# First stage of a decoder layer on one core: rotary rows gathered at half width and turned between key products, eight value blocks given places of their own

## The chip, the cores and the metric

The kernel runs on 1 core of a Trainium2 chip. The metric is the device time of one execution in microseconds (us). A core has TensorE (PE, with its weight loads as PEld), VectorE (DVE), ScalarE (ACT), GpSimd (POOL) and SyncE (SP); each works through its own instructions in order, and they wait for each other by semaphores. DMA queues are fed by SP, ACT and POOL.

## The reference

A decoder layer on 32 sequences of 64 tokens (2048 tokens), hidden size 512, all in float32:

```python
x = x + attention(layernorm(x))                         # 32 heads of 16
x = x + cross_attention(layernorm(x), ctx, pos, mask)   # 32 heads of 128, 8 key/value heads, rotary
x = x + ffn(layernorm(x))                               # 512x512 and sixteen low-rank adapters
# what the first stage of the kernel computes, from ctx alone:
k = (ctx @ Wk).reshape(nb, 64, 8, 128); v = (ctx @ Wv).reshape(nb, 64, 8, 128)
k = k * cos_t[pos] + rotate_half(k) * sin_t[pos]        # cos and sin repeat over the two halves of 128
```

## The kernel before, in words

**Stages.** The first stage (class KeysAndValues) projects the context to rotated keys and to values and writes both to scratch in HBM. The self-attention, the cross-attention (which reads the scratch back) and the adapters follow. Nothing in this change but the first stage and one wait behind it is touched. Every float32 operand of a projection is split: a high part in the matmul's input type (an ACT copy, `_hi`), and the rest (a DVE subtraction, `_lo`). A product is three matmuls per chunk of 128 input channels, hi·hi, hi·lo and lo·hi, over KC = 4 chunks: 12 matmuls of 128x512 (`product3`, L69).

**Blocks.** The 2048 tokens are NB = 4 blocks of 512. A block has KVH = 8 value products (L429; product i is token tile i % 4 and one half of the value columns) and 8 key products (L423; one per head). Block 0 differs from blocks 1 to 3. In block 0 the loads come in, PE makes the values first (`first_values`, L436: four products interleaved chunk by chunk, as the chunks come; then values 4 to 7), then keys 0 and 1, then it transposes the cosine and sine rows of all tokens (L465), and then it makes keys 2 to 7. In blocks 1 to 3, PE alternates a key product and a value product.

**What orders the work around the change.** Everything is written by hand, engine by engine; semaphores tie them.

- SP (L230) issues the loads of context and value weights by chunk in turn, the identity, the other half of the value weights, and after `c_ready` the eight key-weight loads; then, in this order, eight value stores (L256), the context of block 1 (L271), and then a key store and a load of tokens by turns. It waits for `v_copied` before each value store, so what stands behind a value store waits too.
- POOL (L292) gathers the cosine and sine rows by position with sixteen indirect DMAs (L298, 128 tokens each, rows of 256 floats: cos, cos, sin, -sin) once the value weights are there, and then adds the two terms of each rotated key (L304).
- ACT (L332) makes the high parts; then for i = 0 to 7 it copies value block i from PSUM to one of two buffers `v_out` (L330; it waits until the store that last read this buffer is done) and makes the high part of key-weight head i (L320). Then it copies the eight groups of turned rows to `cos_t` and `sin_t` (L345), and makes the high part of context block 1.
- DVE (L394) makes the low parts; then for each key three multiplications by cos and sin (`rotate_terms`, L167 to L171) into one of two buffers `k_out` (it waits until the key store that last read it is done) and into `rb`; in between the low parts of context block 1 (L369).
- A product needs a free PSUM bank. Values 4, 5, 6 and 7 wait for the copies of values 0, 1, 4 and 5 (L430), a key product for the rotation two keys earlier (L424).

Of the kernel before, what the change touches and what calls it, by code (L numbers as in the profile page):

```python
# [173 lines left out]
class KeysAndValues:  # L174


    def __init__(self, nc, m, base, banks, x, norm1, ident, drams, wv1_hi, wv1_lo):
# [17 lines left out]
        v_out = [sb(f"v_out{i}", (148 + 2 * i) * KB, [P, BLOCK]) for i in range(2)]  # L195
        pos = sb("pos", 152 * KB, [P, TILES], mybir.dt.uint32)
# [33 lines left out]
        def sync(sp):  # L230
            for c in range(KC):
                sp.dma_start(c_raw[0][:, c, :], ctx_dram[:, c, 0:BLOCK]).then_inc(c_in0[c], 16)
                sp.dma_start(raw["v"][:, c, 0:BLOCK], wv_dram[:, c, 0:BLOCK]).then_inc(v_raw_in[c], 16)
            sp.dma_start(ident[:, :], ident_dram).then_inc(id_in, 16)
            for c in range(KC):
                sp.dma_start(raw["v"][:, c, BLOCK:NKV], wv_dram[:, c, BLOCK:NKV]).then_inc(v_raw_in[KC + c], 16)
            sp.wait_ge(c_ready, KC)
            for i in range(KVH):
                sp.dma_start(raw["k"][:, :, i * D2:(i + 1) * D2], wk_dram[:, :, i * D2:(i + 1) * D2]).then_inc(k_raw_in[i // 2], 16)
# [9 lines left out]
            def store_keys(b, i):  # L249
                need(sp, k_added, b * KVH + i + 1)  # L250
                sp.dma_start(k_scr[i, ds(b, 1), :, :].rearrange("b p n -> p (b n)"), k_out[i % 2][:, :]).then_inc(k_stored[i % 2], 16)

            def store_values(b, i):
# [3 lines left out]
                             v_out[i % 2][:, :].rearrange("p (g d) -> p g d", d=D2)).then_inc(v_stored[i % 2], 16)  # L257
# [1737 lines left out]
```

## Time and profile before

| | us |
|---|---|
| median of 3 runs (lowest to highest) | 1434.88 (1432.6 to 1436.09) |
| the profiled execution: its own time | 1437.98 |
| its span, first to last instruction | 1436.2 |
| PE busy in the span | 1398.4 (97%) |
| DVE / POOL / ACT busy | 1021.6 / 529.2 / 432.5 |
| stretch of the span that holds block 0 of the first stage | 0 to 65.90 |

Times in the rows are us from the span's start. A matmul's duration in a row is longer than the distance to the next one, since matmuls overlap in the engine; how fast PE goes is read from the distance between starts. An instruction's idle time before it, and what ended it, stand in square brackets.

### The profile page before, as it was taken

How to read it: one execution, taken by the hardware profiler on the slowest of the kernel's cores; microseconds unless marked ns; L12 is line 12 of the kernel's file. 1: busy time of each engine (PE TensorE's matmuls, PEld its weight loads, DVE VectorE, ACT ScalarE, POOL GpSimd, SP SyncE). 2: the span in 40 equal slices, each digit the busy share in tenths (PEclk: the TensorE clock that was granted, in tenths of full speed). 3: DMA queues.
4: the chain of work that ended last, by engine and by line, in shares of the span. 5: the costliest groups of instructions: out<-in, count | busy, mean ns of one | idle time of the engine just before them, and what ended most of it. 6: DMA issues, size and time to landing. Idle time of an engine off the chain costs nothing.

```text
span 1436.2 us, 27963 instructions
## 1 busy us (share of the span) xinstructions
PE 1398.4 (97%) x11616; PEld 1157.3 (81%) x11616; DVE 1021.6 (71%) x1470; ACT 432.5 (30%) x733; POOL 529.2 (37%) x459
## 2 busy tenths in 40 slices
PE   7999999999997889999999999999999999999999
PEld 5788888788886678888888888888888888888787
DVE  3655552788889977777777777767767767778754
ACT  4211133555667333123123123122122122121421
POOL 4322220334443534344344344344344344342231
PEclk9999999999999989999999999999999999999999
DMA  8565330000005102011011011012011012003011
GB/s 248 158 213 167 125 96 8 2 17 25 10 3 148 30 16 75 30 45 46 30 45 51 25 45 59 16 45 60 15 46 59 16 45 60 16 16 115 1 59 59
DMA packets 79116, 84.09 MB, mean 59 GB/s; under 512 B 9824, under 2 KB 50928, under 8 KB 78736
## 3 DMA queue, kind: packets, MB, share of 16 engines
q1 hardware_dynamic: 68976, 63.42, 14.2%
q10 hardware_dynamic: 9216, 16.78, 3.7%
q0 software_dynamic: 800, 2.11, 0.5%
q8 instruction: 94, 1.54, 0.5%
q14 instruction: 30, 0.25, 0.1%
HBM read 59.22 MB, written 23.07 MB: 57 GB/s over the span
## 4 chain that ended last, share of the span: by engine, by line
PE 60%; POOL 3%; DVE 1%; issue 1%; ACT 0%; ACTq 0%
PE p_ps_y L1240 6%; PE p_ps_y L1242 6%; PE p_ps_y L1241 6%; PE p_ps_qk L75 4%; PE p_ps_qk L77 4%; PE p_ps_qk L76 4%; PE p_ps_s L1201 3%; POOL p_wo_lo L1164 3%; PE p_ps_s L1212 2%; PE p_ps_o L75 2%; PE p_ps_s L1242 2%; PE p_ps_s L1241 2%; PE p_ps_s L1240 2%; PE p_ps_o L76 2%; PE p_ps_o L77 2%; PE p_ps_s L1227 2%
## 5 line engine op out<-in xcount | busy, mean ns | idle before, releaser
L1619 POOL TENSOR_TENSOR p_q_rot<-p_q_rot,p_rb 128x512 f32<-128x512 f32 x128 | 167.6, 1309 | 324.7 <-DVE p_rb L171 324.7
L1240 PE MATMUL p_ps_y<-p_wo_hi,p_o_hi 128*128 128x512 f32 x384 | 151.2, 394 | 1.9 <-DVE p_o_lo L1494 1.3
L1241 PE MATMUL p_ps_y<-p_wo_lo,p_o_hi 128*128 128x512 f32 x384 | 149.5, 389 | 0.0
L1242 PE MATMUL p_ps_y<-p_wo_hi,p_o_lo 128*128 128x512 f32 x384 | 149.5, 389 | 0.0
L75 PE MATMUL p_ps_qk<-p_xt_hi,p_wq_hi 128*128 128x512 f32 x312 | 130.3, 418 | 1.0 <-issue 1.0
L999 POOL TENSOR_TENSOR p_pn<-p_p,p_inv 128x512 f32<-128x512 f32 x64 | 66.2, 1066 | 155.2 <-DVE p_inv L889 152.7
L77 PE MATMUL p_ps_qk<-p_xt_hi,p_wq_lo 128*128 128x512 f32 x312 | 122.9, 394 | 0.0
L76 PE MATMUL p_ps_qk<-p_xt_lo,p_wq_hi 128*128 128x512 f32 x312 | 121.9, 391 | 0.0
L1348 ACT ACTIVATE p_pt_hi<-p_ps_s 128x512 fp32r<-128x512 f32 x64 | 38.2, 599 | 255.2 <-PE p_ps_s L1212 255.2
L1503 DVE TENSOR_TENSOR x_sb<-p_ps_y,x_sb 128x512 f32<-128x512 f32 x96 | 66.3, 691 | 68.4 <-PE p_ps_y L1242 67.4
L1354 ACT ACTIVATE p_o_hi<-p_ps_s 128x512 fp32r<-128x512 f32 x64 | 34.8, 595 | 232.2 <-PE p_ps_s L1227 232.2
L304 POOL TENSOR_TENSOR p_k_out<-p_k_out,p_rb 128x512 f32<-128x512 f32 x32 | 44.9, 1402 | 117.7 <-DVE p_rb L171 117.7
L1240 PEld LDWEIGHTS p_ps_y<-p_wo_hi,p_o_hi 128*128 128x128 f32 x384 | 72.1, 188 | 20.0 <-POOL p_wo_lo L1164 3.6
L1625 POOL TENSOR_TENSOR p_v_lo<-p_v_in,p_v_hi 128x512 fp32r<-128x512 f32 x32 | 41.5, 1296 | 116.8 <-ACT p_v_hi L1339 116.8
L1242 PEld LDWEIGHTS p_ps_y<-p_wo_hi,p_o_lo 128*128 128x128 f32 x384 | 72.1, 188 | 15.1
L1241 PEld LDWEIGHTS p_ps_y<-p_wo_lo,p_o_hi 128*128 128x128 f32 x384 | 72.2, 188 | 14.7 <-issue 0.2
L1612 POOL TENSOR_TENSOR p_s<-p_s,p_inv 128x512 f32<-128x512 f32 x64 | 65.6, 1047 | 35.6 <-DVE p_inv L1470 35.6
L169 DVE TENSOR_TENSOR p_q_rot<-p_ps_qk,p_cos_t 128x512 f32<-128x512 f32 x64 | 43.8, 685 | 44.1 <-PE p_ps_qk L77 42.1
L77 PEld LDWEIGHTS p_ps_qk<-p_xt_hi,p_wq_lo 128*128 128x128 f32 x312 | 58.7, 188 | 13.8
L75 PEld LDWEIGHTS p_ps_qk<-p_xt_hi,p_wq_hi 128*128 128x128 f32 x312 | 58.9, 189 | 13.2 <-issue 1.4
L1343 ACT ACTIVATE p_s<-p_s 128x1024 f32<-128x1024 f32 x32 | 34.0, 1062 | 117.7 <-DVE p_s L1462 117.7
L1201 PE MATMUL p_ps_s<-p_k_t,p_q_rot 128*64 128x64 f32 x2048 | 68.2, 226 | 0.5 <-POOL p_q_rot L1619 0.5
(265 smaller groups left out, 3802.2 us busy)
## 6 DMA issues: line engine op xcount, KB each, us to landing
v_scratch<-p_v_out SPq DMA_DIRECT2D x32, 256.0 KB
k_scratch<-p_k_out SPq DMA_DIRECT2D x32, 256.0 KB, 2.1
p_raw<-in_wq SPq DMA_DIRECT2D x32, 256.0 KB, 3.1
p_raw<-in_wo SPq DMA_DIRECT2D x32, 256.0 KB, 2.6
p_k_t<-k_scratch ACTq DMA_DIRECT2D x32, 256.0 KB, 2.6
p_v_in<-v_scratch ACTq DMA_DIRECT2D x32, 256.0 KB, 2.9
x_sb<-in_x SPq DMA_DIRECT2D x16, 256.0 KB, 3.0
out<-p_y SPq DMA_DIRECT2D x16, 256.0 KB, 2.0
```

The costliest lines, as they stand in the source:

```text
L75: nc.tensor.matmul(out, lh, rh, start=(c == 0), stop=False)
L76: nc.tensor.matmul(out, lh, rl, start=False, stop=False)
L77: mm = nc.tensor.matmul(out, ll, rh, start=False, stop=(c == last))
L304: nc.gpsimd.tensor_tensor(k_out[i % 2][:, :], k_out[i % 2][:, :], rb[i % 2][:, :], ALU.add).then_inc(k_added, 1)
L999: nc.gpsimd.tensor_tensor(pn[:, u * PB:(u + 1) * PB, :, :].rearrange("p b j k -> p j b k"), part, scale.unsqueeze(3).broadcast_to([P, HALF ...
L1201: mm = nc.tensor.matmul(ps_s[half][rows, (h // PAIR * UB + j) * SEQ:(h // PAIR * UB + j + 1) * SEQ], q_rot[:, h, cols], k_t[:, cols], star ...
L1240: nc.tensor.matmul(ps_y[t][:, :], oh, w_hi["o"][h][:, :], start=(h == 0), stop=False)
L1241: nc.tensor.matmul(ps_y[t][:, :], oh, w_lo["o"][h][:, :], start=False, stop=False)
L1242: mm = nc.tensor.matmul(ps_y[t][:, :], ol, w_hi["o"][h][:, :], start=False, stop=(h == H - 1))
L1503: nc.vector.tensor_tensor(x[:, tile, :], ps_y[t][:, :], x[:, tile, :], ALU.add).then_inc(y_added, 1)
L1612: nc.gpsimd.tensor_tensor(part, part, inv[:, half * SETS:(half + 1) * SETS].unsqueeze(2).broadcast_to([P, SETS, SEQ]), ALU.mult).then_inc( ...
L1619: nc.gpsimd.tensor_tensor(q_rot[:, h, :], q_rot[:, h, :], rb[:, :], ALU.add).then_inc(q_added, 1)
```

## The change

The table of rotary rows in HBM has 128 floats per position (64 cosines, 64 sines) where it had 256 (each cosine twice, sine and minus sine). The sixteen gathers write 128 floats per token into one tile `rows`, and count on four semaphores, one per block. PE turns the rows of one block with 4 transposes, 16 in all instead of 32, ahead of keys 0, 2, 4 and 6 of block 0. ACT spreads one turned group over both halves of `cos_t` and `sin_t` with four copies of 64x512 (one scaled by -1), 16 copies instead of 8 of 128x512; the copies of groups 1 to 3 stand behind a wait for all eight value stores of block 0 and for the context of block 1.

Value blocks 0 to 7 of block 0 are copied to eight buffers `v_first`, which lie where context block 1's parts are put later. There are four `k_out` buffers instead of two. The first piece of the value weights is loaded by ACT's queue. PE makes the four first hi·hi matmuls of chunk 0 as soon as both high parts are there. On ACT the value copies 0 to 3 come first, and key-weight heads are done two at a time between copies 4 to 7; the key weights are counted on two semaphores of four loads each. On SP, context block 1 is loaded after value store 5.

```diff
+        KOUT = 4
+        k_out = [sb(f"k_out{i}", at * KB, [P, BLOCK]) for i, at in enumerate((50, 60, 62, 146))]
+        rows = sb("rows", 52 * KB, [P, TILES, D2])
...
+        v_first = [sb(f"v_first{i}", (128 + 2 * i) * KB, [P, BLOCK]) for i in range(KVH)]
...
         def sync(sp):
             for c in range(KC):
                 sp.dma_start(c_raw[0][:, c, :], ctx_dram[:, c, 0:BLOCK]).then_inc(c_in0[c], 16)
-                sp.dma_start(raw["v"][:, c, 0:BLOCK], wv_dram[:, c, 0:BLOCK]).then_inc(v_raw_in[c], 16)
+                if c > 0:
+                    sp.dma_start(raw["v"][:, c, 0:BLOCK], wv_dram[:, c, 0:BLOCK]).then_inc(v_raw_in[c], 16)
...
             def first():
                 for i in range(KVH):
                     store_values(0, i)
-                load_context(1)
-                sp.wait_ge(row_copied, 2)
+                    if i == KVH - 3:
+                        load_context(1)
                 for i in range(KVH):
                     store_keys(0, i)
                     load_tokens(i)
...
         def gpsimd(pool):
...
             for t in range(TILES):
-                pool.indirect_dma_start(rows(t), None, table_dram, bass.IndirectOffsetOnAxis(ap=pos[:, t:t + 1], axis=0)).then_inc(row_in, 16)
+                pool.indirect_dma_start(rows[:, t, :], None, table_dram, bass.IndirectOffsetOnAxis(ap=pos[:, t:t + 1], axis=0)).then_inc(row_in[t // TPB], 16)
...
             def copy_values(b, i):
                 need(act, v_done, b * KVH + i + 1)
-                need(act, v_stored[i % 2], (b * (KVH // 2) + i // 2) * 16)
-                nc.scalar.activation(v_out[i % 2][:, :], values_bank(b, i)[:, :], ACT.Copy).then_inc(v_copied, 1)
+                if b > 0:
+                    need(act, v_stored[i % 2], ((b - 1) * (KVH // 2) + i // 2) * 16)
+                nc.scalar.activation(values_out(b, i)[:, :], values_bank(b, i)[:, :], ACT.Copy).then_inc(v_copied, 1)
+
+            def copy_rows(blk):
+
+                act.wait_ge(row_turned, blk + 1)
+                cols, ps = slice(blk * BLOCK, (blk + 1) * BLOCK), ps_r[blk % 2]
+                nc.scalar.activation(cos_t[0:HALF, cols], ps[0:HALF, :], ACT.Copy)
+                nc.scalar.activation(cos_t[HALF:D2, cols], ps[0:HALF, :], ACT.Copy)
+                nc.scalar.activation(sin_t[0:HALF, cols], ps[HALF:D2, :], ACT.Copy)
+                nc.scalar.activation(sin_t[HALF:D2, cols], ps[HALF:D2, :], ACT.Copy, scale=-1.0).then_inc(row_copied, 1)
 
             def first():
+                act.dma_start(raw["v"][:, 0, 0:BLOCK], wv_dram[:, 0, 0:BLOCK]).then_inc(v_raw_in[0], 16)
...
-                for i in range(KVH):
+                for i in range(TPB):
                     copy_values(0, i)
-                    key_weights_hi(i)
-                for n in range(2 * NB):
-                    act.wait_ge(row_turned, n + 1)
-                    dst = (cos_t, sin_t)[n % 2]
-                    nc.scalar.activation(dst[:, (n // 2) * BLOCK:(n // 2 + 1) * BLOCK], ps_r[n % 2][:, :], ACT.Copy).then_inc(row_copied, 1)
+                for i in range(TPB, KVH):
+                    key_weights_hi(2 * (i - TPB))
+                    if i < KVH - 1:
+                        key_weights_hi(2 * (i - TPB) + 1)
+                    copy_values(0, i)
+                copy_rows(0)
+                key_weights_hi(KVH - 1)
+                act.wait_ge(v_first_stored, 16 * KVH)
                 act.wait_ge(c_in, 16)
-                for c in range(KC):
-                    context_hi(1, c)
+                for blk in range(1, NB):
+                    copy_rows(blk)
+                    if blk < NB - 1:
+                        context_hi(1, 2 * (blk - 1))
+                        context_hi(1, 2 * (blk - 1) + 1)
...
             def rotate(b, i):
...
-                need(dve, row_copied, 2 * (b + 1))
+                need(dve, row_copied, b + 1)
                 need(dve, k_added, n - 1)
-                need(dve, k_stored[i % 2], (b * (KVH // 2) + i // 2) * 16)
...
+                need(dve, k_stored[i % KOUT], n // KOUT * 16)
...
             def first_values():
 
+                pe.wait_ge(c_part, 1)
+                pe.wait_ge(part_hi["v"], 1)
+                for i in range(TPB):
+                    nc.tensor.matmul(values_bank(0, i)[:, :], c_hi[0][:, 0, i * P:(i + 1) * P], w_hi["v"][:, 0, 0:BLOCK], start=True, stop=False)
...
+            def turn_rows(blk):
+
+                pe.wait_ge(row_in[blk], 16 * TPB)
+                need(pe, row_copied, blk - 1)
+                for t in range(TPB):
+                    tr = nc.tensor.transpose(ps_r[blk % 2][:, t * P:(t + 1) * P], rows[:, blk * TPB + t, :], ident[:, :])
+                tr.then_inc(row_turned, 1)
 
             def first():
...
-                for i in range(2):
-                    pe.wait_ge(ready["k"], i + 1)
-                    keys(0, i)
                 pe.wait_ge(id_in, 16)
...
-                for i in range(2, KVH):
+                for i in range(KVH):
+                    if i % 2 == 0:
+                        turn_rows(i // 2)
                     pe.wait_ge(ready["k"], i + 1)
                     keys(0, i)
...
-    return np.concatenate([cos, cos, sin, -sin], axis=1)
+    return np.concatenate([cos, sin], axis=1)
```

DVE's first stage keeps its order but for the low parts of context block 1, which come behind rotations 3 to 6 instead of 0 to 3. Behind the stage DVE waits for the stores of three of the four `k_out` buffers where it waited for one of two.

**How instructions move.** On ACT, in block 0 behind the value weights, stood before:

```order
L330 ACTIVATE p_v_out_71<-p_ps_s 128x512 [waits p3_p1_v_done]
L320 ACTIVATE p_wk_hi<-p_raw_k 128x4x128 [waits p3_p1_k_raw_in0]
L330 ACTIVATE p_v_out_72<-p_ps_s 128x512 [waits p3_p1_v_done]
L320 ACTIVATE p_wk_hi<-p_raw_k 128x4x128 [waits p3_p1_k_raw_in0]
L330 ACTIVATE p_v_out_71<-p_ps_s 128x512 [waits p3_p1_v_stored0,p3_p1_v_done]
L320 ACTIVATE p_wk_hi<-p_raw_k 128x4x128 [waits p3_p1_k_raw_in1]
```

and stands now, from the first value copy to the second group of turned rows:

```order
L340 ACTIVATE p_v_first_74<-p_ps_s 128x512 [waits p3_p1_v_done]
...
L340 ACTIVATE p_v_first_77<-p_ps_s 128x512 [waits p3_p1_v_done]
L329 ACTIVATE p_wk_hi<-p_raw_k 128x4x128 [waits p3_p1_k_raw_in0] x2
L340 ACTIVATE p_v_first_78<-p_ps_s 128x512 [waits p3_p1_v_done]
L329 ACTIVATE p_wk_hi<-p_raw_k 128x4x128 [waits p3_p1_k_raw_in0] x2
L340 ACTIVATE p_v_first_79<-p_ps_s 128x512 [waits p3_p1_v_done]
...
L329 ACTIVATE p_wk_hi<-p_raw_k 128x4x128 [waits p3_p1_k_raw_in1]
L340 ACTIVATE p_v_first_81<-p_ps_s 128x512 [waits p3_p1_v_done]
L346 ACTIVATE p_cos_t<-p_ps_y 64x512 [waits p3_p1_row_turned]
...
L329 ACTIVATE p_wk_hi<-p_raw_k 128x4x128 [waits p3_p1_k_raw_in1]
L346 ACTIVATE p_cos_t<-p_ps_y 64x512 [waits p3_p1_row_turned,p3_p1_c_in,p3_p1_v_first_stored]
```

Value copies no longer wait for `v_stored`, two key-weight heads stand ahead of copy 4, and the second group of turned rows has two waits for DMAs. On PE, the rows were turned after two keys, in one piece (ps_y are the banks of the turned rows, ps_s those of the products):

```order
L77 MATMUL p_ps_s<-p_c_hi_67,p_wk_lo 128x512
L465 MATMUL p_ps_y<-ident,p_rows_61 128x128 [waits p3_p1_row_in,p3_p1_id_in]
L465 MATMUL p_ps_y<-ident,p_rows_61 128x128 x7
L465 MATMUL p_ps_y<-ident,p_rows_61 128x128 [waits p3_p1_row_copied]
...
L465 MATMUL p_ps_y<-ident,p_rows_62 128x128 x3
L75 MATMUL p_ps_s<-p_c_hi_67,p_wk_hi 128x512 [waits p3_p1_k_terms,p3_p1_ready_k]
```

and are now turned in four pieces, the first ahead of every key product:

```order
L77 MATMUL p_ps_s<-p_wv_hi,p_c_lo_70 128x512
L486 MATMUL p_ps_y<-ident,p_rows 128x128 [waits p3_p1_row_in0,p3_p1_id_in,p3_p1_v_copied]
L486 MATMUL p_ps_y<-ident,p_rows 128x128 x3
L75 MATMUL p_ps_s<-p_c_hi_68,p_wk_hi 128x512 [waits p3_p1_ready_k]
...
L486 MATMUL p_ps_y<-ident,p_rows 128x128 [waits p3_p1_row_in1]
L486 MATMUL p_ps_y<-ident,p_rows 128x128 x3
L75 MATMUL p_ps_s<-p_c_hi_68,p_wk_hi 128x512 [waits p3_p1_k_terms,p3_p1_ready_k]
...
L486 MATMUL p_ps_y<-ident,p_rows 128x128 [waits p3_p1_row_copied,p3_p1_row_in2]
```

Each piece waits for the gathers of its own block, and the third and fourth for ACT's copies of the first and second.

## Rows read from the trace of the kernel before

**Rows 1.** Stages of the span: busy time of each engine, granted clock, DMA share, GB/s

```profile
core 0: us, PE busy (x) PEld busy (x) DVE busy (x) ACT busy (x) POOL busy (x), PEclk, DMA share, GB/s
0.00:6.69 6.69, 0.00 (x1) 0.03 (x1) 1.53 (x3) 3.17 (x4) 0.95 (x5) 1.00 0.65 201
6.69:24.53 17.84, 17.84 (x72) 14.49 (x72) 7.82 (x12) 8.44 (x15) 7.61 (x8) 1.00 0.94 297
24.53:27.98 3.45, 0.16 (x2) 0.01 (x1) 1.38 (x2) 2.09 (x5) 2.62 (x3) 0.83 0.96 243
27.98:36.18 8.20, 8.20 (x24) 6.52 (x25) 2.08 (x3) 2.62 (x5) 5.68 (x6) 0.66 0.68 187
36.18:41.63 5.45, 5.45 (x26) 4.46 (x24) 0.69 (x1) 1.12 (x2) 0.00 (x0) 1.00 0.56 143
41.63:46.50 4.87, 4.23 (x33) 3.29 (x32) 2.06 (x3) 3.47 (x7) 0.86 (x1) 1.00 0.44 160
46.50:65.90 19.40, 17.27 (x75) 13.27 (x74) 14.90 (x22) 2.96 (x6) 9.10 (x7) 1.00 0.46 150
65.90:240.00 174.10, 174.10 (x790) 143.63 (x789) 90.21 (x150) 39.00 (x69) 38.39 (x30) 1.00 0.41 132
240.00:1436.20 1196.20, 1171.19 (x10605) 971.60 (x10603) 900.94 (x1275) 369.64 (x623) 463.94 (x402) 0.99 0.13 40
```

**Rows 2.** Who PE waited for from 0 to 240: us in total, times, longest

```profile
PE p_ps_s L444 <- DVE p_wv_lo L375: 6.7, 1, 6.7
PE p_ps_s L75 <- ACT p_v_out L330: 3.3, 1, 3.3
PE p_ps_s L75 <- DVE p_rb L171: 2.1, 3, 1.3
PE p_ps_y L465 <- ACT p_cos_t L345: 0.6, 3, 0.3
```

**Rows 3.** Timeline, the first loads on SP, first work on ACT, DVE, PE: start, us

```profile
0.75 0.39 SPq L232 DMA_DIRECT2D p_raw_k<-in_ctx  x1
1.20 0.42 SPq L233 DMA_DIRECT2D p_raw_v<-in_wv  x1
...
3.63 0.63 ACT L309 ACTIVATE p_c_hi<-p_raw_k 128x512 fp32r<-128x512 f32 x1 [1.59 <-DMA p_raw_k<-in_ctx]
5.19 0.63 ACT L315 ACTIVATE p_wv_hi<-p_raw_v 128x512 fp32r<-128x512 f32 x1 [0.93 <-DMA p_raw_v<-in_wv]
...
5.85 0.69 DVE L375 TENSOR_TENSOR p_wv_lo<-p_raw_v,p_wv_hi 128x512 fp32r<-128x512 f32 x1 [0.86 <-ACT p_wv_hi L315]
...
9.79 0.40 PE L445 MATMUL p_ps_s<-p_wv_lo,p_c_hi 128*128 128x512 f32 x1
```

**Rows 4.** Timeline of ACT, value copies and key-weight heads

```profile
17.25 0.60 ACT L330 ACTIVATE p_v_out<-p_ps_s 128x512 f32<-128x512 f32 x1 [2.69 <-PE p_ps_s L446]
...
23.84 0.60 ACT L330 ACTIVATE p_v_out<-p_ps_s 128x512 f32<-128x512 f32 x1 [4.47 <-issue]
24.34 0.62 ACT L320 ACTIVATE p_wk_hi<-p_raw_k 128x512 fp32r<-128x512 f32 x1
24.86 0.59 ACT L330 ACTIVATE p_v_out<-p_ps_s 128x512 f32<-128x512 f32 x1
...
27.32 0.60 ACT L330 ACTIVATE p_v_out<-p_ps_s 128x512 f32<-128x512 f32 x1 [1.36 <-DMA v_scratch<-p_v_out]
```

**Rows 5.** Timeline of PE around the turned rows

```profile
41.63 1.03 PE L465 MATMUL p_ps_y<-ident,p_rows 128*128 128x128 f32 x8
42.91 1.15 PE L465 MATMUL p_ps_y<-ident,p_rows 128*128 128x128 f32 x8 [0.25 <-ACT p_cos_t L345]
```

**Rows 6.** Timeline of DVE, one rotation behind a key store

```profile
60.84 0.69 DVE L169 TENSOR_TENSOR p_k_out<-p_ps_s,p_cos_t 128x512 f32<-128x512 f32 x1 [1.35 <-DMA k_scratch<-p_k_out]
61.54 0.69 DVE L170 TENSOR_TENSOR p_rb<-p_ps_s,p_sin_t 64x512 f32<-64x512 f32 x1
62.25 0.68 DVE L171 TENSOR_TENSOR p_rb<-p_ps_s,p_sin_t 64x512 f32<-64x512 f32 x1
```

**Rows 7.** Timeline of POOL, first and last of the sixteen gathers

```profile
14.78 1.39 POOL L298 DMA_INDIRECT p_rows<-in_table_c,p_pos  x1 [12.76 <-DMA p_raw_v<-in_wv]
...
34.33 0.95 POOL L298 DMA_INDIRECT p_rows<-in_table_c,p_pos  x1 [0.30 <-issue]
```

More of the change, by code:

```diff
@@ L287, in sync @@
             sp.wait_ge(tables_out, 16 * 2 * NB)
+            for i in range(KOUT):
+                sp.wait_ge(k_stored[i], 16 * NB * KVH // KOUT)
+            sp.wait_ge(v_first_stored, 16 * KVH)
             for i in range(2):
-                sp.wait_ge(k_stored[i], 16 * NB * KVH // 2)
-                sp.wait_ge(v_stored[i], 16 * NB * KVH // 2)
+                sp.wait_ge(v_stored[i], 16 * (NB - 1) * KVH // 2)
         def gpsimd(pool):
@@ L294, in gpsimd @@
             pool.wait_ge(pos_in, 16)
-            for n in range(NH * KC):
-                pool.wait_ge(v_raw_in[n], 16)
+            for c in range(KC):
+                pool.wait_ge(v_raw_in[c], 16)
+            pool.wait_ge(v_raw_in[KC], 16 * KC)
             for t in range(TILES):
-                pool.indirect_dma_start(rows(t), None, table_dram, bass.IndirectOffsetOnAxis(ap=pos[:, t:t + 1], axis=0)).then_inc(row_in, 16)
+                pool.indirect_dma_start(rows[:, t, :], None, table_dram, bass.IndirectOffsetOnAxis(ap=pos[:, t:t + 1], axis=0)).then_inc(row_in[t // TPB], 16)
             def body(b):
@@ L303, in body @@
                     need(pool, k_terms, n + 1)
[L304 removed]
+                    nc.gpsimd.tensor_tensor(k_out[i % KOUT][:, :], k_out[i % KOUT][:, :], rb[i % 2][:, :], ALU.add).then_inc(k_added, 1)
             blocks(lambda: body(0), body)
@@ L443, in first_values @@
                         ch, cl, wh, wl = c_hi[0][:, c, tile], c_lo[0][:, c, tile], w_hi["v"][:, c, 0:BLOCK], w_lo["v"][:, c, 0:BLOCK]
-                        nc.tensor.matmul(out, ch, wh, start=(c == 0), stop=False)
+                        if c > 0:
+                            nc.tensor.matmul(out, ch, wh, start=False, stop=False)
                         nc.tensor.matmul(out, ch, wl, start=False, stop=False)
@@ L455, in first @@
                 need(pe, v_copied, TPB)
-                for i in range(2):
-                    pe.wait_ge(ready["k"], i + 1)
-                    keys(0, i)
                 pe.wait_ge(id_in, 16)
-                pe.wait_ge(row_in, 16 * TILES)
-                for n in range(2 * NB):
-                    blk, part = n // 2, n % 2
-                    need(pe, row_copied, n - 1)
-                    for t in range(TPB):
-                        tr = nc.tensor.transpose(ps_r[part][:, t * P:(t + 1) * P], rows(blk * TPB + t)[:, part * D2:(part + 1) * D2], ident[:, :])
-                    tr.then_inc(row_turned, 1)
-                for i in range(2, KVH):
+                for i in range(KVH):
+                    if i % 2 == 0:
+                        turn_rows(i // 2)
                     pe.wait_ge(ready["k"], i + 1)
@@ L923, in _ @@
             need(dve, kv.tables_out, 16 * 2 * NB)
-            need(dve, kv.k_stored[0], 16 * NB * KVH // 2)
+            for stored in kv.k_stored[0:3]:
+                need(dve, stored, 16 * NB * KVH // 4)
             for t in range(TILES):
```

39 lines of the change are left out of this document (19 added, 20 removed).

## The prediction

> **What bounds the kernel now.** I read the stages of the span first. PE is busy 1398 of 1436 us; from 65.90 to 240 it is busy without a gap, and behind 240 it lacks 25 us in places that this change does not touch [rows 1]. So only what PE loses before 65.90, the start of block 1's first key product, can be won, and every us of it should come off the end, since all that follows is released by PE's own progress. Next I read whom PE waited for: four causes before 65.90, none from there to 240 [rows 2]. The reader should lay both over each other, as the stages were cut at PE's events. They add up to 65.90:
>
> - 0 to 6.69: no matmul yet. The first waits for the low part of the value weights [rows 2, 3].
> - 6.69 to 24.53: 72 matmuls (values 0 to 5).
> - 24.53 to 27.98: PE stands still. Value 6 needs the bank of value 4, and ACT's copy of value 4 started only at 27.32, since its buffer was being stored [rows 4].
> - 27.98 to 36.18: 24 matmuls (values 6, 7) in 8.20 us, at a granted clock of 0.66 over the stretch, where 24 at full clock take 5.45 us (36.18 to 41.63, keys 0 and 1) [rows 1]. The clock fell to its lower level, 1.2 GHz, behind the stop.
> - 41.63 to 46.50: the 32 transposes, with some stops for ACT's copies.
> - 46.50 to 65.90: six key products in 19.40 us. Six at full rate are 3 x 5.45 = 16.35. The rest is waiting for DVE's rotations, which wait in turn for a key store to free their buffer, 1.35 us in the row shown [rows 6].
>
> **The change, part by part.** I take each part against this list.
>
> *Start.* The first four matmuls need only high parts now. The one of the weights ends at 5.19 + 0.63 = 5.82, the low part at 5.85 + 0.69 = 6.54, and PE began 0.15 later [rows 3]. That is 0.72 earlier. The weight load leaves first on ACT's queue, not second on SP's: 1.20 - 0.75 = 0.45 earlier. Together 1.2: PE starts at 5.5. Bounds: if the load lands as fast as the context's (3.63 - 0.75 = 2.9 us from issue, where it took 5.19 - 1.20 = 4.0), ACT goes 3.63, 4.26, 4.89 and PE starts at 5.04, a gain of 1.65; if the context's load becomes as slow as the weights' instead, ACT starts at 4.75, ends at 6.01 and PE starts at 6.16, a gain of 0.5. I take the middle, because both loads share the engines either way. PE then runs on: its remaining eight matmuls of chunk 0 wait for a low part about 0.45 earlier than 6.54, when four matmuls are under way. Its first slow matmuls (the spacing turns fast at 9.79, 3.1 us after the start [rows 3]) I leave at the same length.
>
> *Value copies.* Copies 0 to 7 wait for no store. The stop of 3.45 us goes, and the slow patch behind it, 8.20 - 5.45 = 2.75 us. What is late next is the pair of key-weight heads that now stands ahead of copy 4. PE, 1.2 earlier, finishes value 5 at 23.3; for value 6 to start then, ACT must start these two heads by about 21.6 (two at 0.5 spacing and the copy at 0.6). They now need the first four key-weight loads. ACT took the third head at 24.34 with no wait for its load, so that it landed is only proven for 24.34 [rows 4]. DMA moved 297 GB/s to 24.53 [rows 1]; the queue up to the fourth load is 1.0 MB context, 2.1 MB value weights, 0.06 MB identity, 1.05 MB key weights and perhaps 0.3 MB gathers: 4.5 MB, or 15 us at that rate, 17 with the first latency. So I cost it at nothing, and keep 3.1 us (21.6 held up to 24.34, plus the copy) and a slow patch for a rival.
>
> *Turned rows.* 32 transposes took 4.87 us, of which 3 short stops 0.6 [rows 1, 2]; eight in a piece take 1.15 [rows 5]. Sixteen are 2.1, and with 0.07 for each of four changes between transposes and products 2.4. Gain 2.45. Bounds: 2.75 with no change costs, 0.3 if a piece of four costs what eight do. The stops for ACT go, since two keys (5.45 us) lie between pieces and ACT's four copies take some 4 x 0.5 to 0.6: no row shows a 64x512 copy on ACT, but DVE took 0.69 for both 128x512 and 64x512 [rows 6], so I count a full one each. ACT has 1.12 us of work in 36.18 to 41.63 [rows 1]; eight more copies there hide.
>
> *Keys.* With four buffers a rotation never waits for a store just issued. It is 0.69 + 0.70 + 0.70 = 2.1 us, with a context part (0.6) at four of eight 2.7, under the 2.72 of a key product. I take the whole 19.40 - 16.35 = 3.05 as won; the other bound is nothing. The tightest place is the first: the last key-weight head now waits for ACT's first row copies, DVE does its low part before rotation 0, and so this rotation ends at about 28.8 + 0.6 + 2.0 + 0.6 + 0.7 + 2.1 = 34.8, when PE, at 28.8 + 0.6 + 5.45 = 34.85, begins piece 1 and then key 2.
>
> *Waits added.* PE's first piece needs four gathers. They are issued from 14.8 on, one each 1.25 us [rows 7], so by about 19.5; PE asks at 28.8. ACT's second group waits for all eight stores and the context: 5.3 MB of loads, 1.0 of gathers, 2.1 of stores and 1.0 of context, 9.4 MB, at 280 GB/s landed near 35; it is needed at PE's fourth piece, near 46.9, and for block 1's rotations. SP has nothing ahead of the value stores that was not there. Narrower rows take a MB off the DMA engines, which hides. The other wait on DVE behind the stage is for stores of about the same time: nothing.
>
> **Sum.** 1.2 + 3.45 + 2.75 + 2.45 + 3.05 = 12.9. Check, laid out anew: 5.5, + 17.84 = 23.3, + 5.45 = 28.8, + 2.4 + 4 x 5.45 = 53.0, against 65.90. From the profiled execution's 1437.98 that gives 1425.1; the median lies 3.1 below that execution, so 1434.88 - 12.9 = **1422.0**.
>
> **Rivals.**
>
> 1. *Key weights late on ACT.* The stores no longer hold each other back, and crowd the loads. ACT stands at the first pair of heads, copy 4 behind it, PE at value 6. The Trainium skill, page DMA: Bandwidth & Descriptors, section Issuing engines are not separate DMA queues, says that DMAs of all queues run on the same 16 engines and interleave; the DMA share of 0.94 to 0.96 [rows 1] agrees. For it: that share. Against: the loads were issued before the stores. Up to 3.1 us and the 2.75 patch stay: gain 7.0, **1427.9**.
> 2. *Gathers late, the other side.* PE's first piece stands ahead of every key. If the first four gathers land at L, PE waits L - 28.8 and pays the 2.75 patch. The gain is gone at L = 38.9; it is slower by more than 4.3 us (0.3%, about what a measurement can tell) from L = 43.2. At L = 45: 16.2 + 2.75 - 12.9 = 6 slower, **1441**. For it: stores and context crowd the same engines earlier than before. Against: all sixteen had landed by 41.63 [rows 5], the last issued at 34.33 [rows 7].
> 3. *Pieces of transposes let the clock fall.* Each would be followed by a slow patch of 2.75: four make 11.0, gain 1.9, **1433.0**. Against: 4.87 us of nothing but transposes stand at a clock of 1.00, and so do the keys behind them [rows 1]. The Trainium skill, page TensorE: Matmul & The Clock Gate, section Part 4: PE-mode transpose, has such a rule: transposes do not count as busy for the clock. By that rule the patches would be there; the row speaks against it.
> 4. *Rotations still wait,* for POOL's additions or by the tight first place: up to 3.05 stays, gain 9.9, **1425**. It lies inside the forecast's range.
> 5. *The change works and the gain is given back later.* PE has no gap in which something could be waited for from 65.90 to 240 [rows 1], and its waits behind are on engines that move along. Then about 1434.
>
> **How the numbers follow.** Forecast with rival 4: 82%. Rival 1: 8%. Rival 2: 5%, of it 2 beyond 43.2 and 3 near no change. Rival 3: 2%. Rival 5: 3%, of it 1 slower. Faster by over 0.3%: 82 + 8 = 90%. Within: 3 + 2 + 2 = 7%. Slower: 3%. Range: the largest gain, with both upper bounds, is 13.65, or 1421.2, and the runs of before scatter by 2 about their median: low end 1419. High end: rival 1 at 1427.9, or the forecast without key gain and with the low bounds of start and rows (12.9 - 3.05 - 0.7 - 2.15 = 7.0), the same value, and 1.6 for scatter: 1429.5.
>
> **What would show it.** PE's first matmul near 5.5; no stop between values 5 and 6 and no clock under 1.00 between 9 and 60; no wait of ACT for a store among copies 4 to 7; four pieces of transposes of about 0.6 us, 5.5 apart; keys 2.72 apart; block 1's first key near 53.0; behind it each event 12.9 earlier. A stop of PE at L486 would be rival 2, at L75 before value 6 rival 1, matmuls 0.43 apart behind a piece rival 3. If block 1's first key comes near 53 and the end does not move, rival 5.

## The result: faster by 10 us

| us | before | after |
|---|---|---|
| median (lowest to highest), 5 runs each | 1434.88 (1432.6 to 1437.84) | 1424.88 (1423.42 to 1427.05) |
| ratio, 95% interval | | 0.9926 [0.9911, 0.9941] |
| the profiled execution | 1437.98 | 1423.42 |
| its span | 1436.2 | 1421.6 |
| PE busy | 1398.4 (97%) | 1389.5 (98%) |
| DVE / POOL / ACT busy | 1021.6 / 529.2 / 432.5 | 1021.8 / 530.1 / 437.6 |
| block 1's first key product starts | 65.90 | 53.26 |

The kernel is faster, and inside the range; the forecast of 1422.0 was 2.9 too low. The same stages as in [rows 1], cut at the same events of PE, in the profile after:

```profile
core 0: us, PE busy (x) PEld busy (x) DVE busy (x) ACT busy (x) POOL busy (x), PEclk, DMA share, GB/s
0.00:5.98 5.98, 0.00 (x0) 0.03 (x1) 0.63 (x2) 2.58 (x4) 0.95 (x5) 1.00 0.63 205
5.98:23.82 17.84, 17.84 (x73) 14.66 (x74) 9.50 (x16) 10.77 (x19) 8.44 (x8) 1.00 1.01 316
23.82:29.22 5.40, 5.40 (x25) 4.42 (x24) 1.99 (x3) 2.75 (x5) 4.18 (x5) 1.00 0.94 215
29.22:53.26 24.04, 23.95 (x113) 19.66 (x112) 17.46 (x26) 12.89 (x22) 13.89 (x12) 1.00 0.56 183
53.26:240.00 186.74, 186.74 (x972) 154.10 (x971) 93.62 (x155) 43.44 (x77) 38.96 (x30) 1.00 0.38 123
```

PE starts at 5.98 and is busy to 53.26 and on to 240, but for 0.09 us. The clock column can't be trusted at the start, where it says 1.00: these rows show PE's matmuls 0.43 us apart, the lower level of 1.2 GHz, up to 9.02, and about 0.23 apart from there on, as in before from 9.79 on [rows 3].

```profile
8.25 0.63 PE L477 MATMUL p_ps_s<-p_wv_hi,p_c_lo 128*128 128x512 f32 x1
8.68 0.50 PE L476 MATMUL p_ps_s<-p_wv_lo,p_c_hi 128*128 128x512 f32 x1
9.02 0.39 PE L477 MATMUL p_ps_s<-p_wv_hi,p_c_lo 128*128 128x512 f32 x1
```

Behind that the clock is 1.00 to 240. Of the four waits of [rows 2] one is left, from 0 to 240:

```profile
PE p_ps_s L467 <- ACT p_wv_hi L324: 6.0, 1, 6.0
```

The timeline of the first work (answers to [rows 3]) and of ACT's last value copies and first row copies (to [rows 4]):

```profile
4.69 0.63 ACT L318 ACTIVATE p_c_hi<-p_raw_k 128x512 fp32r<-128x512 f32 x1 [2.21 <-DMA p_raw_k<-in_ctx]
5.22 0.61 ACT L324 ACTIVATE p_wv_hi<-p_raw_v 128x512 fp32r<-128x512 f32 x1
...
5.98 2.04 PE L467 MATMUL p_ps_s<-p_wv_hi,p_c_hi 128*128 128x512 f32 x4 [5.98 <-ACT p_wv_hi L324]
```

```profile
26.70 0.60 ACT L340 ACTIVATE p_v_first<-p_ps_s 128x512 f32<-128x512 f32 x1 [1.08 <-PE p_ps_s L77]
27.19 0.62 ACT L329 ACTIVATE p_wk_hi<-p_raw_k 128x512 fp32r<-128x512 f32 x1
29.42 0.60 ACT L340 ACTIVATE p_v_first<-p_ps_s 128x512 f32<-128x512 f32 x1 [1.61 <-PE p_ps_s L77]
29.91 0.58 ACT L346 ACTIVATE p_cos_t<-p_ps_y 64x512 f32<-64x512 f32 x1
...
32.33 0.63 ACT L329 ACTIVATE p_wk_hi<-p_raw_k 128x512 fp32r<-128x512 f32 x1
```

ACT could take the first chunk of the context at 4.69, not at 3.63, and the weights' at once behind it: both first loads, now issued together, take about the same time. ACT's copies wait for PE alone, no longer for a store.

Three sums follow. Start: 6.69 - 5.98 = 0.7. Values: 96 matmuls took 36.18 - 6.69 = 29.49 and take 29.22 - 5.98 = 23.24, 6.25 less. Keys and turned rows: 65.90 - 36.18 = 29.72 against 53.26 - 29.22 = 24.04, 5.68 less. Together 12.64. Behind block 1's first key the profiled executions took 1436.2 - 65.90 = 1370.3 and 1421.6 - 53.26 = 1368.3.

### The profile page after: what moved, and what is told of

It reads as the page before. It is cut to its first block, busy times and chain, and to the rows that moved or that the text cites. A ratio compares the mean times of both kernels' runs of the same rounds, so it can differ in the third digit from the quotient of the medians.

```text
span 1421.6 us, 27933 instructions
## 1 busy us (share of the span) xinstructions
PE 1389.5 (98%) x11600; PEld 1151.6 (81%) x11600; DVE 1021.8 (72%) x1470; ACT 437.6 (31%) x741; POOL 530.1 (37%) x459
## 4 chain that ended last, share of the span: by engine, by line
PE 61%; DVE 2%; POOL 1%; issue 1%; ACT 0%; ACTq 0%
PE p_ps_y L1272 6%; PE p_ps_y L1274 6%; PE p_ps_y L1273 6%; PE p_ps_s L1233 4%; PE p_ps_qk L75 4%; PE p_ps_qk L77 4%; PE p_ps_qk L76 4%; PE p_ps_s L1244 2%; PE p_ps_o L75 2%; PE p_ps_s L1274 2%; PE p_ps_s L1273 2%; PE p_ps_s L1272 2%; PE p_ps_o L76 2%; PE p_ps_o L77 2%; PE p_ps_s L75 2%; PE p_ps_s L77 2%
```

## The experiments

Twelve runs of nine kernels, in three groups, each on another chip. The runs of before beside them had medians of 1435.33 (17 runs), 1436.72 (19, one of them at 4872.9) and 1435.68 (17). "The landmark" is the start of block 1's first key product in the trace.

| run | edit | time, us | ratio to before [95%] | landmark |
|---|---|---|---|---|
| again | none | 1424.59 | 0.9927 [0.991, 0.9944] | 53.49 |
| only_places | before, with the eight places alone | 1436.19 | 1.0004 [0.9995, 1.0014] | 64.75 |
| alt | the changed kernel with ACT's old order | 1425.66, one run | | 53.52 |
| alt_two | alt, and two value buffers | 1426.04 | 0.9939 [0.9917, 0.9961] | 55.03 |
| kout2 | two key buffers | 1434.19 | 0.9974 [0.9952, 0.9995] | 63.48 |
| onepiece | transposes in one piece | 1432.49 | 0.9976 [0.9959, 0.9993] | 62.24 |
| twice | each transpose twice | 1431.46, one run | | 59.42 |
| sp_load | first weight load on SP's queue | 1434.59, one run | | 61.99 |
| again_b | none | 1424.63 | 0.9926 [0.9911, 0.9942] | 54.05 |
| kout2_b | as kout2 | 1424.2 | 0.9926 [0.9908, 0.9944] | 54.16 |
| onepiece_b | as onepiece | 1431.53 | 0.9969 [0.9957, 0.9981] | 59.55 |
| warm | matmuls of zeros ahead of the first | 1423.22 | 0.9919 [0.9904, 0.9934] | 52.68 |

### The change once more

> The changed kernel once more, unchanged. Theory A (all that follows block 1's first key is carried along by PE): the stage is 12.6 us shorter in every execution (65.90 to 53.26 in the two traces), so the median comes out 12 to 13 below that of before, and the 10.0 of the first comparison was scatter. Theory B (some 2 to 3 us are given back behind the stage): the median difference is again about 10, and the first key of block 1 starts at 53.3 all the same.

Measured: 1424.59 (1423.6 to 1426.77, 6 runs), 10.7 under before, with the landmark 12.4 earlier. The stage gives what it gave; the medians again differ by less than the stage does. More on this below.

### The eight places alone

```diff
-    need(act, v_stored[i % 2], (b * (KVH // 2) + i // 2) * 16)
-    nc.scalar.activation(v_out[i % 2][:, :], ...
+    if b > 0:
+        need(act, v_stored[i % 2], ((b - 1) * (KVH // 2) + i // 2) * 16)
+    nc.scalar.activation(values_out(b, i)[:, :], ...
```

> The kernel before with one part of the change alone: eight value buffers in block 0. Theory A (each term of the sum stands by itself): the stop of 3.45 and the slow patch of 2.75 go, block 1's first key moves from 65.90 to 59.7, the time falls by 6.2. Theory C (the next wait is near): PE now asks for all turned rows at 35.4 instead of 41.6, and the sixteenth gather is issued at 34.33 and takes 2 us or more to land, so PE stands at L472 or so for about 2 to 3 us; first key of block 1 at 61.7 to 63, time lower by 3 to 4 only. No clock under 1.00 in values 6 and 7 by either.

Measured: no gain, 12 runs from 1435.5 to 1437.55. PE's waits before the landmark, and two of its stages (values; transposes):

```profile
PE p_ps_s L453 <- DVE p_wv_lo L384: 6.3, 1, 6.3
PE p_ps_y L474 <- DMA p_rows<-in_table_c,p_pos: 2.9, 1, 2.9
PE p_ps_s L75 <- DVE p_rb L171: 2.0, 3, 1.3
```

```profile
6.30:30.84 24.54, 24.54 (x97) 20.09 (x97) 11.51 (x17) 13.79 (x24) 13.55 (x12) 1.00 0.98 292
...
39.32:46.50 7.18, 6.96 (x37) 5.54 (x38) 2.07 (x3) 4.95 (x9) 1.26 (x1) 0.76 0.02 7
```

The stop ahead of value 6 is gone: the values take 24.54, where they took 29.49, 4.95 less. PE is then at the transposes earlier than the sixteen gathers have landed, stands 2.9 us for them from 36.4 on, and does them at a lowered clock, which rises again while they run: granted were 0.51 from 39.32 to 40.50 and 1.00 from 43.50 on, and PE did nothing but transposes between. The values also cost more here than in the changed kernel (24.54 against 23.24), because in this execution the first matmuls stayed 0.43 apart up to 12.25, not 9.02. The next key starts at 45.41, where in before it was 46.50: of 4.95 and the 0.4 of the start 1.1 is left. So the wait for stores hid a wait for gathers, and with all sixteen of them asked for at once the first could not be won without the second. In the changed kernel, where only four gathers are needed for a piece, PE never waits for one.

### ACT's order, and two value buffers

```diff
-    for i in range(TPB):
+    for i in range(KVH):
         copy_values(0, i)
-    for i in range(TPB, KVH):
...
+        key_weights_hi(i)
     copy_rows(0)
-    key_weights_hi(KVH - 1)
```

> The changed kernel with ACT's old order in block 0 (copy of a value, then one key-weight head, by turns) and still eight value buffers. If the order of ACT is worth nothing by itself: PE has no stop and the first key of block 1 starts at 53.3. Rival: the first four key-weight loads land later than copy 1 is due (17.2), the first head holds copy 1 and those behind it up; PE stops only if that reaches copy 4 at 21.3, that is if they land after 20.

Measured: 1425.66, no stop, landmark 53.52, inside the 53.26 to 54.05 of the three traces of the unchanged kernel. By this one run ACT's order is worth nothing by itself.

alt_two also puts `v_out[i % 2]` back for block 0, with its waits.

> As the run with ACT's old order, but with two value buffers in block 0 as before: against that run it differs in the buffers alone. Theory A: the stop before value 6 comes back with 3 to 4 us, and the slow patch with 2.7 behind it; first key of block 1 about 6 later than there, near 59.5; time about 6 above the changed kernel. Rival (the stores were slow only because the gathers moved twice the bytes beside them): the stop is under 1.5 us, without a slow patch.

Measured: 1426.04 (1425.6 to 1428.85, 4 runs). PE's one stop, and ACT's waits for stores behind it:

```profile
25.68 0.50 PE L75 MATMUL p_ps_s<-p_wv_hi,p_c_hi 128*128 128x512 f32 x1 [0.70 <-ACT p_v_out L338]
```

```profile
21.85 0.60 ACT L338 ACTIVATE p_v_out<-p_ps_s 128x512 f32<-128x512 f32 x1 [2.19 <-DMA v_scratch<-p_v_out]
...
26.66 0.60 ACT L338 ACTIVATE p_v_out<-p_ps_s 128x512 f32<-128x512 f32 x1 [0.52 <-DMA v_scratch<-p_v_out]
...
31.60 0.60 ACT L338 ACTIVATE p_v_out<-p_ps_s 128x512 f32<-128x512 f32 x1 [1.71 <-DMA v_scratch<-p_v_out]
```

ACT still waits for stores, but 2.19 and 0.52 us, where it stood 4.47 and 1.36 in before [rows 4]. PE stops once, for 0.70 instead of 3.45, and its clock does not fall. The landmark is 1.5 later than with eight places. So in the changed kernel the places are worth 1.5 us, not the 6.2 that the sum gives them. That is the rival of the expectation in size, but not its reason: only_places has gathers as wide as before's, and its first two value stores landed 3.7 and 4.0 us after their issue, those of alt_two 3.6 and 3.4. In before the first store was issued at 17.87, and ACT got into its buffer only at 23.84, 5.97 later. That trace lacks many semaphore records, as those of a later section do, so a part of its stop may belong to that one execution; how much is not known. Its key-weight loads, which stand ahead of the stores on SP, also left later (11.93, against 10.90 and 11.04), and the other loads' order was not tried alone.

### Transposes in one piece

```diff
-    if i % 2 == 0:
-        turn_rows(i // 2)
+    if i == 2:
+        for blk in range(NB):
+            turn_rows(blk)
```

ACT then copies the four groups one behind the other, and the context parts behind them. Twice run.

> The changed kernel with its 16 transposes in one piece behind key 1, and ACT's sixteen row copies in one piece too. Theory A (pieces between keys hide ACT's copies): piece 3 waits for the four copies of group 0 (2.4 us) and piece 4 for those of group 1, so the transposes take 6.0 instead of 2.4, the first key of block 1 starts at 56.9, time up by 3.6. Rival (transposes are the only cost): the same 53.3.

> All sixteen transposes in one piece behind key 1, once more, beside the unchanged changed kernel. Theory L: if the chip is clean, TensorE waits twice for ScalarE to copy a group of rows (2.4 us each, less the 0.6 of a group of transposes) and once for rotation 0, some 3.5 us together and no slow patch: block 1's first key at 57, time 1428. Theory M: as in the first run of it, signals late between 28 and 38, stops of 3.6 and 1.8 us, then matmuls at the lower clock, key at 62.2, 1432.5.

Measured: 1432.49 (10 runs), landmark 62.24; then 1431.53 (10 runs), landmark 59.55. PE in the second:

```profile
35.51 1.03 PE L484 MATMUL p_ps_y<-ident,p_rows 128*128 128x128 f32 x8
38.68 0.63 PE L484 MATMUL p_ps_y<-ident,p_rows 128*128 128x128 f32 x4 [2.14 <-ACT p_sin_t L349]
41.11 0.83 PE L484 MATMUL p_ps_y<-ident,p_rows 128*128 128x128 f32 x4 [1.80 <-ACT p_sin_t L349]
...
42.16 0.63 PE L76 MATMUL p_ps_s<-p_c_lo,p_wk_hi 128*128 128x512 f32 x1
42.59 0.63 PE L77 MATMUL p_ps_s<-p_c_hi,p_wk_lo 128*128 128x512 f32 x1
```

Two waits for ACT's copies (2.4 us a group) make 3.94, and behind them matmuls are 0.43 apart up to 44.73, the lower clock, which the expectation had not (57 and 1428). Behind that PE loses nothing more:

```profile
41.59:45.00 3.41, 3.41 (x10) 2.69 (x9) 1.26 (x2) 3.34 (x6) 1.79 (x2) 0.53 0.50 154
45.00:59.55 14.55, 14.55 (x65) 12.01 (x64) 12.51 (x19) 3.00 (x6) 7.01 (x5) 1.00 0.46 155
```

Against again_b on the same chip the landmark is 5.50 later, the time 6.9. The transposes take 41.59 - 35.51 = 6.08 with their waits, and key 2 takes 4.34 instead of 2.72; keys 3 to 7 are 2.72 apart. So with the new copies, four to a group, spreading the pieces saves 5.5 us of stage. It is no share of the 12.64, since before's old copies, two to a group, let its one piece stop for 0.6 only [rows 2].

### Two key buffers

```diff
-KOUT = 4
+KOUT = 2
```

> The changed kernel with two key buffers instead of four. Theory A (the whole 3.05 us of the old stretch of keys was waiting for stores): PE stops between keys again, in sum about 3, first key of block 1 at 56.3. Rival D (a piece of transposes every two keys gives the stores 0.5 more time a pair): a pair of keys takes 6.05 on PE against 2.1 of rotation, 1.3 to 1.8 of addition and 2.5 of store for the same buffer, about 6.3; stops of 0.3 a pair, first key of block 1 at 54.3.

Measured: 1434.19 (1427.71 to 1435.9, 10 runs), landmark 63.48, nearly the whole gain lost. The expectation had the landmark at 54.3 to 56.3, and from key 4 on the keys start as far apart as in the changed kernel. ACT's rows show another thing:

```profile
25.55 0.60 ACT L340 ACTIVATE p_v_first<-p_ps_s 128x512 f32<-128x512 f32 x1 [1.53 <-PE p_ps_s L77]
26.05 1.14 ACT L329 ACTIVATE p_wk_hi<-p_raw_k 128x512 fp32r<-128x512 f32 x2
34.03 0.60 ACT L340 ACTIVATE p_v_first<-p_ps_s 128x512 f32<-128x512 f32 x1 [6.84 <-remote]
```

ACT stands 6.84 us ahead of the copy of value 6, and the profile finds no releaser ("remote"). The copy waits for PE's signal of the finished product alone.

### Each transpose twice; the first load on SP's queue

```diff
-    for t in range(TPB):
+    for t in range(2 * TPB):
```

> The changed kernel with every transpose issued twice (32 in all, as many as before, in pieces of eight; the result is the same). Theory A: four times 0.55 more on PE, first key of block 1 at 55.5. Rival (transposes lie in slack that PE has beside DVE's rotations): less than 1 us more.

```diff
-    if c > 0:
-        sp.dma_start(raw["v"][:, c, 0:BLOCK], ...
+    sp.dma_start(raw["v"][:, c, 0:BLOCK], ...
...
-    act.dma_start(raw["v"][:, 0, 0:BLOCK], ...
```

> The changed kernel with the first piece of the value weights back on SP's queue, second in its row, and the early hi-hi matmuls kept. Theory E (both loads share the DMA engines, so the other queue wins nothing): context part on ACT at 3.63 as before, weights at 5.19, first matmul at 5.97 where the changed kernel had 5.98. Theory F (the forecast's: the queue is worth 0.45): first matmul at 6.4.

Measured: twice 1431.46, pieces of eight taking 1.03 where those of four take 0.60, so a transpose more costs 0.11; behind three of these pieces keys are at full clock too (matmuls 0.23 apart), and behind the second PE first stands 2.39 us for a rotation and falls to 0.43 apart at 40.87. sp_load 1434.59, PE's first matmul at 5.96, as in the changed kernel: the other queue for the first load shows no gain, and the 0.7 us of the start come from beginning with the high parts. One trace decides this only roughly, since the ten traces that load as the changed kernel does start from 5.62 to 6.42; but in all ten the context's first chunk is taken at 4.33 to 5.13, in sp_load at 4.19, and in before at 3.63. But both lost more behind 30 us than their edit explains. In sp_load:

```profile
28.60 0.60 ACT L339 ACTIVATE p_v_first<-p_ps_s 128x512 f32<-128x512 f32 x1 [2.70 <-remote]
...
34.31 0.60 ACT L339 ACTIVATE p_v_first<-p_ps_s 128x512 f32<-128x512 f32 x1 [4.59 <-remote]
```

```profile
29.28 0.39 PE L77 MATMUL p_ps_s<-p_wv_hi,p_c_lo 128*128 128x512 f32 x1
29.51 0.60 PE L484 MATMUL p_ps_y<-ident,p_rows 128*128 128x128 f32 x4
```

The last product of values ends at 29.67 by PE's row, and the copy that waits for it starts at 34.31. The trace also records when each semaphore was raised. Laid beside the ends of the matmuls that raise it (us; blank where no piece stands between value 7 and key 0):

```
                 value 7         first piece     key 0           key 1
                 ends  signal    ends  signal    ends  signal    ends  signal
sp_load          29.67 34.28     30.11 36.42     32.88 37.92     35.60 38.05
kout2            30.51 36.90     30.95 36.96     33.72 37.08     38.82 38.83
twice            29.98 30.13     30.86 32.99     33.59 37.32     36.32 37.44
onepiece         30.49 30.57                     33.21 36.95     35.93 37.75
before           36.34 37.85                     39.06 39.08     41.79 41.80
after            29.38 29.40     29.82 29.83     32.59 32.61     35.31 35.33
kout2_b          each signal within 0.02 of its matmul's end
```

In all four runs of the second group PE's signals came up to 6.4 us behind the matmul and then in a bunch: two products that take 2.7 us each were signalled 0.13 apart. The waiting engines started with the signal, so the lateness is real for them. It ended between 37 and 38 each time. Just these traces also lack semaphore records: between 14 and 38 us they hold 192 to 199, those of the other two groups and of after 509 to 575, with no signal of PE late. The trace of before holds 145, the fewest of all. So its stage of 65.90, from which every term was taken, may hold some of this disturbance too.

### The same kernels on another chip

> The changed kernel as it is, beside the two variants that lost more than their edit explains (two key buffers, transposes in one piece). In the traces of those two, TensorE's signals of finished products came to ScalarE up to 6 us behind the end of the matmul, and several at once (key 0's and key 1's 0.13 us apart in the run with the first load on SyncE's queue), between 27 and 38 us; in every trace of the changed kernel so far each signal stands 0.015 us behind its matmul's end. Those disturbed traces were all taken on one chip, the clean ones on others. Theory L (late signals go with the chip or the execution, whatever the kernel): where the variants show them again here, this kernel shows them too, block 1's first key is at 59 or later and the time 1430 or more. Theory M (they go with the kernel's own program): this run is as before, 1424.6, block 1's first key at 53.4, whatever the variants show.

> Two key buffers instead of four, once more, now beside the unchanged changed kernel on the same chip. Theory L: if this chip and execution are clean, ScalarE's copies of values 6 and 7 start with the end of their products (26.7, 29.4), and what the two buffers cost shows by itself: rotations 2 to 7 wait for the store before last, at most the 3.05 us of my key term, block 1's first key between 53.4 and 56.5, time 1424.6 to 1427.6. Theory M: copy 6 is late again (34.0), key at 63.5, about 1434.

Measured: again_b 1424.63, landmark 54.05; kout2_b 1424.2 (4 runs), landmark 54.16. The kernel that took 1434.19 is 10 us faster on this chip, its code unchanged. Late signals do not come with the kernel's code alone, they came with that chip or its executions (Theory L); whether the unchanged kernel would have met them there was not run. And two key buffers cost nothing in the changed kernel. DVE in kout2_b:

```profile
40.10 0.69 DVE L169 TENSOR_TENSOR p_k_out<-p_ps_s,p_cos_t 128x512 f32<-128x512 f32 x1 [1.38 <-DMA k_scratch<-p_k_out]
...
42.50 0.69 DVE L169 TENSOR_TENSOR p_k_out<-p_ps_s,p_cos_t 128x512 f32<-128x512 f32 x1 [0.31 <-PE p_ps_s L77]
...
51.79 0.69 DVE L169 TENSOR_TENSOR p_k_out<-p_ps_s,p_cos_t 128x512 f32<-128x512 f32 x1 [0.39 <-DMA k_scratch<-p_k_out]
```

A rotation still waits 1.38 us for a store, about as in [rows 6]. But DVE has time for it now: the rotation behind that one waits for PE again, and PE stops nowhere.

### Zeros ahead of the first matmul

```diff
+    pe.wait_ge(k_terms, 1)
+    for i in range(5):
+        nc.tensor.matmul(ps_r[0][:, 0:256], warm[:, 0:P], warm[:, 0:256], start=True, stop=True)
```

> The changed kernel with five matmuls of zeros (128x256) on TensorE while the first loads are under way, into a bank that is free until the transposes; VectorE makes the zeros. In the changed kernel the first matmuls are 0.43 us apart (1.2 GHz) from 5.98 on and fast only behind some seven of them. Theory W: the clock is granted by what the engine did just before, so the real matmuls start fast: 7 x 0.2 = 1.4 us less, block 1's first key at 52.0, time 1423.2. Theory N: TensorE is idle again between the zeros and the first real one, or the early matmuls wait for chunks 1 to 3 of context and weights anyway, and nothing is gained: 1424.6.

Measured: 1423.22 (1422.37 to 1426.04, 6 runs). PE's first rows of again_b, then of warm:

```profile
6.20 2.05 PE L467 MATMUL p_ps_s<-p_wv_hi,p_c_hi 128*128 128x512 f32 x4 [6.20 <-ACT p_wv_hi L324]
8.05 0.63 PE L476 MATMUL p_ps_s<-p_wv_lo,p_c_hi 128*128 128x512 f32 x1
8.47 0.63 PE L477 MATMUL p_ps_s<-p_wv_hi,p_c_lo 128*128 128x512 f32 x1
...
10.97 0.40 PE L475 MATMUL p_ps_s<-p_wv_hi,p_c_hi 128*128 128x512 f32 x1
```

```profile
1.47 4.64 PE L468 MATMUL p_ps_y<-p_warm 128*128 128x256 f32 x10 [1.47 <-DVE p_warm L422]
6.13 1.84 PE L472 MATMUL p_ps_s<-p_wv_hi,p_c_hi 128*128 128x512 f32 x4
7.80 0.40 PE L481 MATMUL p_ps_s<-p_wv_lo,p_c_hi 128*128 128x512 f32 x1
8.04 0.39 PE L482 MATMUL p_ps_s<-p_wv_hi,p_c_lo 128*128 128x512 f32 x1
```

The first four real matmuls are still 0.43 apart; those from 7.80 on are 0.23 apart, and chunk 1's first one starts at 9.63 instead of 10.97, so the landmark is 1.37 earlier, as Theory W has it. But where the spacing turns fast differs between traces of the unchanged kernel: 9.02 (after), 9.53 (again), 10.52 (again_b), with landmarks of 53.26, 53.49 and 54.05. Against these warm's 52.68 is 0.6 to 1.4 earlier. The median is 1.41 under again_b's on the same chip. That is the best time of the study, but the intervals of the two ratios overlap: the traces show a gain but not its size, and the runs alone do not prove it.

## Why the prediction was right, and where its steps were not

**The size of the stage.** Forecast 12.9, measured 12.64. By its terms: start 1.2, measured 0.7; value stop and slow patch 3.45 + 2.75 = 6.2, measured 6.25; rows and keys 2.45 + 3.05 = 5.5, measured 5.68. (The 5.50 between onepiece_b and again_b is another sum, and the likeness is chance.)

**Start.** The step that failed is the 0.45 for ACT's queue: sp_load starts as early without it, as far as one trace tells. The load did not gain on the context's; both landed at once and later, which was the lower bound's reasoning (6.16; measured 5.98).

**Value copies.** The size was right, the cause only in part. The eight places alone bring nothing (only_places), since the gathers are next; in the changed kernel they carry 1.5 (alt_two), so the good fit of 6.2 and 6.25 is in part luck. I asked what is late next and named the key-weight heads, but with all changes made at once I did not see that the wider gathers would have been the next wait without the new pieces. Rival 1 (heads late) did not come: ACT took them without a wait. Nor rival 2: PE never waited for a gather of the first group. The 3.1 us that rival 1 keeps do not follow from its own terms: 24.34 - 21.6 is 2.7, and 21.6 had the copy's 0.6 in it.

**Turned rows.** Four pieces of 0.60, 5.9 to 6.3 apart; I had written 5.5, which forgets the piece itself. Beside eight keys of 2.72 they take 24.04 - 21.80 = 2.24, where I had 2.4. In it is a third of a us that the tight first place costs: rotation 0 ends at 35.69, and key 2 starts at 35.84, 0.69 behind its piece, where the other keys start 0.35 behind theirs. Rival 3 is refuted: pieces, and the keys behind them, are at a clock of 1.00, and in only_places the clock rose while PE did nothing but transposes. The Trainium skill, page TensorE: Matmul & The Clock Gate, section Part 4: PE-mode transpose, says that transposes do not count as busy for the clock; by that rule these stretches would have had slow patches, and this case's traces do not agree (0.51 to 1.00 in only_places, during 32 float32 transposes).

**Keys.** The term was right in size, and its reason only in part. I gave the 3.05 to four buffers ("a rotation never waits for a store just issued"). Between keys 2 and 7 PE stopped three times in before, and DVE's rows tell why:

```profile
47.93 0.69 DVE L369 TENSOR_TENSOR p_c_lo<-p_raw_v,p_c_hi 128x512 fp32r<-128x512 f32 x1 [2.39 <-ACT p_c_hi L309]
50.78 0.47 PE L75 MATMUL p_ps_s<-p_c_hi,p_wk_hi 128*128 128x512 f32 x1 [1.29 <-DVE p_rb L171]
54.66 0.69 DVE L169 TENSOR_TENSOR p_k_out<-p_ps_s,p_cos_t 128x512 f32<-128x512 f32 x1 [0.58 <-DMA k_scratch<-p_k_out]
56.91 0.47 PE L75 MATMUL p_ps_s<-p_c_hi,p_wk_hi 128*128 128x512 f32 x1 [0.40 <-DVE p_rb L171]
63.08 0.47 PE L75 MATMUL p_ps_s<-p_c_hi,p_wk_hi 128*128 128x512 f32 x1 [0.44 <-DVE p_rb L171]
```

The largest stop, 1.29, was not behind a store: DVE had a context part ahead of rotation 1 and stood 2.39 for ACT's high part of it. The two others, 0.84 together, follow rotations that waited for stores (0.58, and 1.35 in [rows 6]). So the step that failed is the reading of the whole 3.05 as waits for stores. None of the three stops comes in kout2_b, which has two buffers and the pieces, nor in onepiece_b, which has four buffers and one piece. Neither buffers nor pieces are thus needed by themselves. Both runs also do the context parts behind rotations 3 to 6 instead of 0 to 3, which is what the largest stop points at; that was not tried alone, so what removed these stops stays open.

**From stage to median.** 12.9 was taken off the median as if every execution of before had the profiled one's stage. The profiled executions differ by 14.56, the medians by 10.0 and, in the two repetitions, 10.7 and 11.05. Part is scatter behind the stage: the traces without late signals, eight of changed kernels and only_places, took 1367.9 to 1371.0 there. A part of that scatter goes with the granted clock, which falls to 0.50 in one to four places behind 240: kout2_b and after, with 10.2 us at 0.50 in all, took 1367.9 and 1368.4, onepiece_b with 20.5 us took 1370.9, before with 17.1 us 1370.3. Before took 1370.3; its median execution, if its stage were 65.90 long, would have had 1434.88 - 1.8 - 65.90 = 1367.2 there, less than any seen. only_places points the same way: its landmark is 1.15 earlier than before's, yet its median is no lower. So I think that the usual stage of before is one or two us shorter than its profiled one, in which signals of PE were late by 0.76 and 1.51 us and most semaphore records from 14 to 38 us are missing. The 2 to 3 us by which the medians differ less than the sum would then lie in the stage that it starts from. This is argued; there is no second trace of before.

## What to carry to other kernels

Ask of every wait that is removed how long the waiting engine would stand for the next thing: here the stop for stores and the one for gathers lay over each other, and removing the first alone gave 0 of 10 us. A side job with a consumer on another engine (transposes, then copies, then rotations) can be cut into pieces with a product or two of the main work between them; in the changed kernel, whose copies are slower than its transposes, one piece cost 5.5 us of stage, and two key buffers in place of four cost nothing. A stage's gain is taken from two single executions: look for missing records in both before adding it up. And before a variant's loss is explained, run it again beside the base on the same chip: one here cost 10 us on one chip and nothing on another.

## What the runs showed of the hardware

- PE's signals can come up to 6.4 us late and in a bunch, with the matmuls themselves on time. It came on one chip in four kernels, by up to 1.5 us in the trace of before, and only in traces that miss records. The DMA share does not tell it: from 28 to 38 us it was 0.56 to 0.71 in the four, and 0.63 and 0.68 in after and again_b, which have no late signal. The Trainium skill, page NOTIFIC — the notification-queue block, section 7.1, says that the block which writes the profiler's records holds back an engine rather than lose a record inside the block; no run here shows whether that is the cause.
- Matmuls of zeros raise PE's clock: behind five of them (ten records, 4.64 us) four real ones still ran at 1.2 GHz, and those from 7.80 us on at 2.4 GHz, where again_b reached it at 10.52.
- Float32 transposes keep PE's clock up, and raise it: 0.51 to 1.00 in only_places, with nothing else on PE.
- ACT takes 0.59 us for 64x512 and 0.60 for 128x512: half the partitions save nothing, as assumed.
